# Delta attention on one core: the query sums move to TensorE, and the newest chunk's errors get a way of their own

## The chip, the cores and the metric

The program runs on one core of one Trainium2 chip, as one launch that computes eight sublayers in a row. The metric is the device time of the launch in microseconds (us). Engines are PE (TensorE), DVE (VectorE), ACT (ScalarE), POOL (GpSimd) and SP (SyncE, which issues the DMAs). All data of the stage in question is fp32.

## The reference, cut to what matters

The changed stage is the seventh sublayer, a gated delta rule. Per batch entry and head it carries a 128x128 state S through the sequence:

```
y   = S k_t                       # what the state answers to the key
err = y - v_t
S   = a_t * S - (b_t * err) k_t^T
o_t = S q_t                       # the output, read with the query
```

In this program the batch has 4 entries of 256 steps, and the width 256 is spread over 16 heads of 128, so there are 64 lanes (head x batch entry). k, q and v come from projections, a causal convolution of four taps and a SiLU; a and b are sigmoids. The outputs are normalized, gated and projected back.

## The kernel before, in words

`delta_attention` works in chunk form. The 256 steps are 4 blocks of 64 (`NBLK`); a block is two half-blocks of 32 steps (`NO`, index o), each of them four chunks of 8 steps (`NI`, index jj; `ci = o*NI + jj`). In a block come, in this order:

- heads: projections, convolution and SiLU for 16 heads, on PE, ACT, DVE and POOL, interleaved with the norm, gate and output projection of the block before (`heads_and_norm`);
- Gram matrices of keys with keys and queries (`gram`, L2046), scaled by -beta into GR (L2410), scattered to DRAM chunk by chunk and read back by SP in broadcast form into M, one of two rooms per chunk (L1853, L1863);
- for each half-block: transposing the state (`state_t`, L2058) and multiplying it with keys and queries (`columns`, L2068) into F (L2331), key rows (`key_rows`), then the four chunks, then the update of S (`update`, L2120, added by DVE in L2491).

For each chunk, POOL's `prepare` builds the decay products DD (L1976), DC, DF, scales F by them (L1999), subtracts V (L2000, semaphore `fp_d`) and multiplies the query half of M by DD (L2002, `mq_d`). Between two chunks it decays the errors W found so far (L2015, `wdec_d`). DVE's `chunk` multiplies the key half of M by DD (L2439), waits for `fp_d` and for `rest_mm`, forms the base in a PSUM bank (L2431, L2432; L2430 in the first chunk), and runs seven key steps of a product and an add (L2454, L2456), since each step's error depends on the earlier ones. It writes W (L2460, `w_d`), and then forms the outputs in bank 5: a base, and eight steps of a product (L2471) and an add (L2478). ACT copies bank 5 to V (L2379).

PE's part between two chunks is a turn (16 transposes of W, L2088, copied by ACT in L2351) and `rest` (L2101): 64 small matmuls, seen as 128 instructions, that carry all errors of the half-block so far to the next chunk's columns. `rest_mm` releases DVE's base of the next chunk.

Each engine runs its instructions in the order in which its function is written; engines meet only at the semaphores. Nothing is planned or scheduled by a table. In the second half-block of each block PE also computes four gate matrices per chunk (`gate`, L2131).

## Time and profile before

| | us |
|---|---|
| median of 3 runs | 2733.68 (2719.57 to 2734.51) |
| the profiled execution's own time | 2720.65 |
| its span, first to last instruction | 2718.9 |

The delta stage takes from about 986 to 2340 us of the span. The page's totals are over all eight sublayers. A row of a view names a source line, the engine, the operation, output and inputs with their shapes, how often it ran, its busy time and the mean of one, and what released the engine after its idle time. A matmul of fp32 shows as two instructions. The granted clock is a share of full speed: 1.00 is 2.4 GHz and 0.50 is 1.2 GHz.

### The profile page before, as it was taken

The numbers are of one execution on the slowest core, as the hardware profiler recorded it, in microseconds if no ns is written. First come the engines' busy times: TensorE is split into PE (matmuls) and PEld (weight loads), VectorE is DVE, ScalarE is ACT, GpSimd is POOL, SyncE is SP. The second block draws the span as 40 slices with busy tenths as digits, with TensorE's granted clock in tenths as the row PEclk, the third lists the DMA queues.
The fourth block names the chain that finished last, engine by engine and source line by source line (L and its number), as shares of the span: only waits on it lengthen the run. The fifth ranks groups of instructions, "written<-read, shape, count | busy, mean of one in ns | idle before, by whom it ended". The sixth has DMA issues, their size and how long they took to land. (4 is left out here: it accounts for less than half of the span.)

```text
span 2718.9 us, 42746 instructions
## 1 busy us (share of the span) xinstructions
PE 2081.5 (77%) x15844; PEld 1636.3 (60%) x15856; DVE 1592.5 (59%) x3191; ACT 1141.1 (42%) x2723; POOL 1175.9 (43%) x996
## 2 busy tenths in 40 slices
PE   7597449978988968657896578955689656768798
PEld 5364126656566857646776567755568655546586
DVE  2223732246664339668776787766778677546533
ACT  3112311136464428434464344743446434325433
POOL 0222022210004535968339683386733877300254
PEclk9698769979998979767797677976779757789899
DMA  8422022210007023422223222232222332020340
GB/s 282 125 24 53 0 69 43 24 38 2 22 2 231 0 34 109 126 95 94 86 74 125 96 94 86 74 119 101 94 77 80 111 114 93 32 56 2 93 138 15
DMA packets 137426, 212.96 MB, mean 78 GB/s; under 512 B 61184, under 2 KB 113680, under 8 KB 132112
## 3 DMA queue, kind: packets, MB, share of 16 engines
q1 hardware_dynamic: 129072, 200.11, 23.1%
q0 software_dynamic: 8160, 10.26, 2.4%
q8 instruction: 122, 2.00, 0.3%
q14 instruction: 72, 0.59, 0.1%
HBM read 187.97 MB, written 22.37 MB: 77 GB/s over the span
## 5 line engine op out<-in xcount | busy, mean ns | idle before, releaser
L2088 PE MATMUL PS<-ident,XT 128*128 128x128 f32 x512 | 112.8, 402 | 258.2 <-DVE XT L2460 245.5
L2402 DVE SCALAR_TENSOR_TENSOR XT<-M_delta,CW_delta,XT 128x256 f32<-128x256 f32 x576 | 249.9, 495 | 70.2 <-ACT M_delta L2271 40.6
L2088 PEld LDWEIGHTS PS<-ident,XT 128*128 128x128 f32 x512 | 90.4, 208 | 277.6 <-DVE XT L2460 132.7
L2037 PE MATMUL PS<-XP_delta,X 128*128 128x268 f32 (+1 forms) x1024 | 241.6, 388 | 5.5 <-DMA X<-in_L_attn_b_heads 5.5
L2037 PEld LDWEIGHTS PS<-XP_delta,X 128*128 128x128 f32 x1024 | 192.7, 189 | 55.7 <-issue 11.4
L1541 PE MATMUL PS<-XP_rffn,UW_rffn 128*128 128x512 f32 x816 | 194.6, 395 | 5.5 <-POOL UW_rffn L1495 4.6
L1976 POOL TENSOR_TENSOR DD_delta<-DD_delta,A_delta 128x64 f32<-128x64 f32 (+6 forms) x224 | 169.9, 759 | 39.2 <-ACT A_delta L2359 19.5
L1541 PEld LDWEIGHTS PS<-XP_rffn,UW_rffn 128*128 128x128 f32 x816 | 155.5, 191 | 39.5 <-issue 6.8
L1273 ACT ACTIVATE PR_attn<-PS,NM_attn 128x256 f32<-128x256 f32 (+1 forms) x384 | 130.7, 448 | 103.6 <-DVE NM_attn L1343 103.6
L1495 POOL TENSOR_TENSOR UW_rffn<-W_rffn,UW_rffn 128x512 fp32r<-128x512 f32 x34 | 44.1, 1298 | 296.0 <-ACT UW_rffn L1602 296.0
L561 POOL DMA_INDIRECT sums<-XS_moe,token_moe x46 | 71.7, 1559 | 221.0 <-ACT XS_moe L661 205.8
L2002 POOL TENSOR_TENSOR M_delta<-M_delta,DD_delta 128x2304 f32<-128x2304 f32 x32 | 164.9, 5154 | 0.0
L1663 DVE TENSOR_TENSOR SU_rffn<-PS,CB_rffn 128x512 f32<-128x512 f32 x68 | 47.0, 691 | 179.8 <-PE PS L1541 158.4
L2373 ACT ACTIVATE S_delta<-S_delta,AO_delta 128x128 f32<-128x128 f32 x512 | 152.0, 389 | 0.0
L2351 ACT COPY KQ_delta<-PS 128x512 f32<-128x512 f32 x128 | 73.3, 585 | 183.5 <-PE PS L2088 183.5
L2068 PE MATMUL PS<-KQ_delta,TR_delta 128*128 128x64 f32 x1024 | 137.7, 282 | 13.3 <-DVE TR_delta L2419 13.1
L2101 PEld LDWEIGHTS PS<-XN,KQ_delta 16*128 16x128 f32 (+2 forms) x3072 | 142.3, 284 | 7.1 <-issue 7.1
L2101 PE MATMUL PS<-XN,KQ_delta 16*128 16x16 f32 (+2 forms) x3072 | 144.9, 336 | 0.0
L2068 PEld LDWEIGHTS PS<-KQ_delta,TR_delta 128*128 128x128 f32 x1024 | 132.9, 203 | 17.6 <-DVE TR_delta L2419 17.6
L1504 POOL TENSOR_TENSOR HP_rffn<-HF_rffn,HP_rffn 128x512 fp32r<-128x512 f32 x68 | 92.7, 1381 | 115.9 <-ACT HP_rffn L1625 115.9
L1918 POOL TENSOR_SCALAR XT<-M_delta,CW_delta,CB_delta 128x256 f32<-128x256 f32 x64 | 51.7, 808 | 164.4 <-ACT M_delta L2271 164.4
L1343 DVE TENSOR_REDUCE NM_attn<-PS 128x4 f32<-128x512 f32 (+1 forms) x144 | 95.0, 684 | 47.3 <-PE PS L1155 47.3
(414 smaller groups left out, 5068.6 us busy)
## 6 DMA issues: line engine op xcount, KB each, us to landing
M_delta<-gram_delta SPq DMA_DIRECT2D x32, 2304.0 KB, 8.7
X<-in_L_attn_b_heads SPq DMA_DIRECT2D x64, 512.0 KB, 3.4
EW<-in_L_ffn_w SPq DMA_DIRECT2D x24, 512.0 KB, 10.0
CB_rffn<-routes_rffn SPq DMA_DIRECT2D x20, 512.0 KB, 22.4
XN<-in_L_attn_b_outs SPq DMA_DIRECT2D x16, 512.0 KB, 3.6
F_delta<-in_L_attn_b_outs SPq DMA_DIRECT2D x4, 2048.0 KB, 8.5
W_rffn<-in_L_ffn_tiles SPq DMA_DIRECT2D x4, 1536.0 KB, 11.6
slots<-pad SPq DMA_DIRECT2D x2, 2967.0 KB, 14.7
```

What stands on the lines that cost most here:

```text
L1273: last = nc.scalar.activation(PR[:, u % (2 * ROWS), j * w:(j + 1) * w], PS[:, r, j * w:(j + 1) * w], ACT.Exp, bias=NM[:, u % (2 * ROWS), j ...
L1343: nc.vector.tensor_reduce(NM[:, u % (2 * ROWS), 0:per], PS[:, r, :].rearrange("p (h j) -> p h j", h=per), AX.X, ALU.max, negate=True).then ...
L1504: nc.gpsimd.tensor_tensor(HP[1][:, r, x], HF[:, n, :], HP[0][:, r, x], ALU.subtract).then_inc(hl_d, 1)
L1541: last = nc.tensor.matmul(PS[:, 4 + 2 * n + q, :], UW[qw][:, r, (q * KD + k) * P:(q * KD + k + 1) * P], XP[qx][:, k, n * NB:(n + 1) * NB], ...
L1976: last = nc.gpsimd.tensor_tensor(DD[:, :, tri(t - 1) + 1:tri(t)], DD[:, :, tri(t):tri(t + 1)], step(t).broadcast_to([P, BH, C - t]), ALU.mult)
L2002: nc.gpsimd.tensor_tensor(q, q, by_h(DD[:]), ALU.mult).then_inc(mq_d, 1)
L2037: last = nc.tensor.matmul(PS[:, 1 + i, 0:B * (WIN - halo)], WH[:, r, i, k, :], XP[:, k, :, n * BT + halo:n * BT + WIN], start=(k == 0), st ...
L2068: last = nc.tensor.matmul(PS[:, 5 * (g % 2), i * 2 * OC:(i + 1) * 2 * OC].rearrange("p (q t) -> p q t", q=2), TR[:, g % 3, i * P:(i + 1) * ...
L2088: last = nc.tensor.transpose(PS[:, 6 + r % 2, i * P:(i + 1) * P], W[:, B * h:B * (h + 1), :], core.ident[:])
L2101: last = nc.tensor.matmul(PS[:, 1 + b, h * 2 * C:(h + 1) * 2 * C].rearrange("p (q t) -> p q t", q=2), WT(o)[rows, h, :], GR[rows, o, h].re ...
L2373: last = nc.scalar.activation(S[:, lane, :], S[:, lane, :], ACT.Copy, scale=AO[:, lane:lane + 1])
L2402: nc.vector.scalar_tensor_tensor(TMP[:, r, i], RAW[:, r, i, :, tau:tau + BT], CW[:, i, h, tau:tau + 1], TMP[:, r, i], ALU.mult, ALU.add).t ...
```

## The change

- DVE no longer adds up the outputs. Its eight products with the query half of M are written back into M, and PE sums them in bank 5 with identity matmuls (`add_steps`), behind two more that bring in F and the query term TQ (`add_first`). ACT copies the bank one chunk later (`answer`).
- The base of the queries (TQ) is formed by DVE ahead of the key steps.
- The errors of the newest chunk go to the next chunk by `newest`: DVE writes them to WN, PE turns them with four transposes, ACT copies them to NEW, and 16 matmuls multiply them with GN, a Gram matrix of one chunk's keys with the next chunk's keys and queries. GN is made once per half-block by `cross_gram` (48 matmuls on PE, three copies and twelve scalings on ACT), and POOL clears what belongs to other batch entries (`same_lanes`) before each use, so that it is block-diagonal.
- The turn and `rest` now handle only older chunks, for chunks 2 and 3, in banks that four matmuls first set to zero. `rest` runs in four tiers with a wait between them. There are three turns per half-block instead of four. ACT copies WN to W (`wc_d`).
- POOL still multiplies the query half of M by DD.
- beta is computed a second time in another layout at the start of the stage, stored to DRAM and read back. The scratch tiles of the norms become one tile.

```diff
+            def same_lanes(n, o, jj):
+
+                pool.wait_ge(cg_d, base_of(n)["cg_d"] + rests(o, jj) + 1)
+                g = GN[:, jj].rearrange("p (i b w) -> p i b w", i=4, b=B)
+                nc.gpsimd.tensor_tensor(g, g, SAME[:].unsqueeze(1).unsqueeze(3).broadcast_to([P, 4, B, 2 * C]),
+                                        ALU.mult).then_inc(gn_d, 1)
...
                     if jj:
-                        pool.wait_ge(wt_mm, z["wt_mm"] + NR * ci)
+                        pool.wait_ge(wc_d, z["wc_d"] + rests(o, jj))
                         r = W[:, :, 0:jj * C]
                         nc.gpsimd.tensor_tensor(r, r, AJ[:, :, jj:jj + 1].broadcast_to([P, BH, jj * C]),
                                                 ALU.mult).then_inc(wdec_d, 1)
                         pool.wait_ge(wdec_d, z["wdec_d"] + rests(o, jj))
+                    if jj + 1 < NI:
+                        same_lanes(n, o, jj)
...
             def rest(n, o, jj):
...
-                for h in range(H):
...
+                for k in range(4):
+                    nc.tensor.matmul(PS[:, 1 + k, 0:2 * C * H], XP[:, 0, 0, 0:1].broadcast_to([P, P]), XP[:, 0, 0, 0:2 * C * H],
+                                     start=True, stop=False)
+                pe.wait_ge(wt_d, z["wt_d"] + NR * (TURNS * o + jj - 1))
+                for y in range(4):
+                    if y:
+                        pe.wait_ge(tier, z["tier"] + 4 * (2 * o + jj - 2) + y)
...
+            def newest(n, o, jj):
+
+                z = base_of(n)
+                x = rests(o, jj - 1)
+                for i in range(4):
+                    last = nc.tensor.transpose(PS[:, 6, i * P:(i + 1) * P], WN[:, i * P:(i + 1) * P], core.ident[:])
+                last.then_inc(nw_mm, 1)
...
+                for i in range(4):
+                    for k in range(4):
+                        rows, at = slice(OC * k, OC * (k + 1)), slice(i * 2 * B * C, (i + 1) * 2 * B * C)
+                        last = nc.tensor.matmul(PS[:, 1 + k, at], NEW[rows, i], GN[rows, jj - 1, at], start=jj == 1,
+                                                stop=jj == 1 or i == 3)
                 last.then_inc(rest_mm, 1)
...
+            def add_steps(n, ci):
+
+                z = base_of(n)
+                for t in range(C):
+                    pe.wait_ge(qm_d, z["qm_d"] + C * ci + t + 1)
+                    last = nc.tensor.matmul(FQ[:, :, :, t:], core.ident[:], M[:, ci % 2, :, 1, :, tri(t):tri(t + 1)],
+                                            start=False, stop=t == C - 1)
+                last.then_inc(q_d, 1)
...
+                        if jj:
+                            add_steps(n, ci - 1)
+                        if 1 <= jj < NI - 1:
+                            pe.wait_ge(wdec_d, z["wdec_d"] + rests(o, jj))
+                            for r in range(NR):
+                                turn(n, TURNS * o + jj - 1, r)
+                            rest(n, o, jj + 1)
+                        add_first(n, ci)
                         pe.wait_ge(w_d, z["w_d"] + ci + 1)
...
-            cuts = [0, 0, 21, 42, BH]
+            cuts = [0, 20, 32, 44, BH]
...
                 dve.wait_ge(mq_d, z["mq_d"] + ci + 1)
...
+                for t in range(C):
+                    x = q[:, :, :, tri(t):tri(t + 1)]
+                    nc.vector.tensor_tensor(x, x, by_h(FK[:, :, t:t + 1].broadcast_to([P, BH, C - t])), ALU.mult).then_inc(qm_d, 1)
```

How the instructions stand on PE's queue between two chunks, before (L2088 is the turn, L2101 `rest`):

```order
L2078 MATMUL PS<-ident,KQ_delta 128x128 x16
L2088 MATMUL PS<-ident,XT 128x128 x16
L2101 MATMUL PS<-XN,KQ_delta 128x16 x64
L2088 MATMUL PS<-ident,XT 128x128 x16
L2101 MATMUL PS<-XN,KQ_delta 128x16 x64
```

And in the changed kernel, from the end of chunk 0's sums to the errors of chunk 1 (L2134 is the turn, L2163 the zeroing, L2174 `rest`, L2206 and L2209 `add_first`, L2185 and L2195 `newest`, L2216 `add_steps`):

```order
L2134 MATMUL PS<-ident,XT 128x128 x16
L2163 MATMUL PS<-XP_delta 128x256 x4
L2174 MATMUL PS<-XN,KQ_delta 128x16 x64
L2206 MATMUL PS<-F_delta,ident 128x512
L2209 MATMUL PS<-TR_delta,ident 128x512
L2185 MATMUL PS<-ident,TR_delta 128x128 x4
L2195 MATMUL PS<-GN_delta,TR_delta 128x64 x16
L2216 MATMUL PS<-M_delta,ident 128x512
L2216 MATMUL PS<-M_delta,ident 128x64x7
```

The matmuls that release the next chunk (L2195) come last, behind the turn, `rest` and the sums of F and TQ. On POOL's queue of the changed kernel, between the q product of chunk 1 and the decays of chunk 2, the masking of GN (L2007) is new, and nothing has gone:

```order
L2046 TENSOR_TENSOR M_delta<-M_delta,DD_delta 128x16x144
L2059 TENSOR_TENSOR XT<-XT,AJ_delta 128x64x8
L2007 TENSOR_TENSOR GN_delta<-GN_delta,SAME_delta 128x256
L2019 TENSOR_TENSOR DD_delta<-DD_delta,A_delta 128x64
L2019 TENSOR_TENSOR DD_delta<-DD_delta,A_delta 128x64x2
```

L2046 is the old L2002, L2059 the old L2015 and L2019 the old L1976.

## Rows read from the trace of the kernel before

**Rows 1.** The page: engine totals, and two of its groups (busy us, mean ns).

```profile
PE 2081.5 (77%) x15844; PEld 1636.3 (60%) x15856; DVE 1592.5 (59%) x3191; ACT 1141.1 (42%) x2723; POOL 1175.9 (43%) x996
...
L2351 ACT COPY KQ_delta<-PS 128x512 f32<-128x512 f32 x128 | 73.3, 585 | 183.5 <-PE PS L2088 183.5
...
L2101 PE MATMUL PS<-XN,KQ_delta 16*128 16x16 f32 (+2 forms) x3072 | 144.9, 336 | 0.0
```

**Rows 2.** Busy times in stretches: us, then busy us by engine, clock, DMA.

```profile
core 0: us, PE busy (x) PEld busy (x) DVE busy (x) ACT busy (x) POOL busy (x), PEclk, DMA share, GB/s
1110.00:1195.00 85.00, 36.34 (x521) 32.47 (x509) 76.16 (x145) 34.55 (x100) 80.78 (x59) 0.58 0.33 109
```

**Rows 3.** Groups of POOL in one period, 1130.90 to 1151.95 us (busy, mean; idle).

```profile
L1976 POOL TENSOR_TENSOR DD_delta<-DD_delta,A_delta 128x64 f32<-128x64 f32 (+6 forms) x7 | 5.3, 757 | 0.6
L2002 POOL TENSOR_TENSOR M_delta<-M_delta,DD_delta 128x2304 f32<-128x2304 f32 x1 | 5.1, 5074 | 0.0
L2000 POOL TENSOR_TENSOR F_delta<-F_delta,V_delta 128x512 f32<-128x512 f32 x1 | 3.5, 3454 | 0.1
L1999 POOL TENSOR_TENSOR F_delta<-F_delta,DF_delta 128x512 f32<-128x512 f32 x2 | 2.4, 1196 | 0.2
L1992 POOL TENSOR_TENSOR DF_delta<-DC_delta,PJ_delta 128x576 f32<-128x576 f32 x1 | 1.2, 1182 | 0.1
L1985 POOL TENSOR_TENSOR DC_delta<-DD_delta,A_delta 128x512 f32<-128x512 f32 x1 | 1.2, 1156 | 0.1
L2015 POOL TENSOR_TENSOR XT<-XT,AJ_delta 128x512 f32<-128x512 f32 x1 | 1.1, 1149 | 0.1
L1990 POOL TENSOR_TENSOR PJ_delta<-AJ_delta 128x64 f32<-128x64 f32 x1 | 0.3, 301 | 0.1
```

**Rows 4.** Groups of DVE in the same period.

```profile
L2478 DVE TENSOR_TENSOR PS<-PS,TR_delta 128x512 f32<-128x512 f32 (+7 forms) x8 | 3.7, 458 | 0.0
L2471 DVE TENSOR_TENSOR TR_delta<-M_delta,PS 128x512 f32<-128x512 f32 (+7 forms) x8 | 3.6, 462 | 0.0
...
L2431 DVE TENSOR_TENSOR PS<-PS,DC_delta 128x512 f32<-128x512 f32 x2 | 1.4, 695 | 1.2 <-POOL F_delta L2000 1.2
```

**Rows 5.** PE in order of time (start, length), then clock in two stretches.

```profile
1143.26 3.76 PE L2088 MATMUL PS<-ident,XT 128*128 128x128 f32 x16 [9.37 <-DVE XT L2460]
...
1234.79 3.72 PE L2131 MATMUL PS<-XP_delta,XN 128*128 128x256 f32 x16 [1.40 <-ACT KQ_delta L2345]
...
1288.63 7.03 PE L2101 MATMUL PS<-XN,KQ_delta 24*128 24x16 f32 x128
1295.59 6.74 PE L2131 MATMUL PS<-XP_delta,XN 128*128 128x256 f32 x16
...
1311.59 2.09 PE L2120 MATMUL PS<-KQ_delta 32*128 32x128 f32 x32
...
1316.28 1.17 PE L2120 MATMUL PS<-KQ_delta 32*128 32x128 f32 x32 [0.68 <-DVE S_delta L2491]
...
2270.26 3.76 PE L2101 MATMUL PS<-XN,KQ_delta 8*128 8x16 f32 x128
...
1246.00:1250.00 4.00, 4.00 (x80) 0.50 0.27 74
2270.00:2274.00 4.00, 4.00 (x133) 1.00 0.01 4
```

**Rows 6.** DVE in order of time at the ends of both half-blocks.

```profile
1185.51 0.69 DVE L2460 TENSOR_TENSOR XT<-PS,X 128x512 f32<-128x512 f32 x1
...
1198.31 2.29 DVE L2491 TENSOR_TENSOR S_delta<-S_delta,PS 128x2048 f32<-128x2048 f32 x1 [2.29 <-PE PS L2120]
...
1304.39 0.69 DVE L2460 TENSOR_TENSOR XT<-PS,X 128x512 f32<-128x512 f32 x1
...
1317.51 2.29 DVE L2491 TENSOR_TENSOR S_delta<-S_delta,PS 128x2048 f32<-128x2048 f32 x1 [1.38 <-PE PS L2120]
```

**Rows 7.** One line's instructions over the span: ns min/median/max.

```profile
L2000 POOL TENSOR_TENSOR F_delta<-F_delta,V_delta x32: 1250/1284/3474, 1111.5 to 2320.9; 128x512 f32<-128x512 f32 x32
L1958 POOL TENSOR_TENSOR X<-X,A_delta x56: 1101/1127/1162, 1095.5 to 2227.0; 128x256 f32<-128x256 f32 x56
```

More of the change, by code:

```diff
@@ L1694, in delta_attention @@
     NR = 4
+    TURNS = NI - 1
     PAIRS = C * (C + 1) // 2
@@ L1784, in _ @@
             last.then_inc(z_mm, 1)
+            for n in range(NH):
+                for k in range(KD):
+                    last = nc.tensor.matmul(PS[0:H, 1 + n, :], WB[:, k, :], XT[:, k, n * NB:(n + 1) * NB],
+                                            start=(k == 0), stop=(k == KD - 1))
+            last.then_inc(row_mm, 1)
         @block.scalar
@@ L1790, in _ @@
             nc.scalar.activation(NBETA[:], NBETA[:], ACT.Sigmoid).then_inc(beta_d, 1)
+            act.wait_ge(row_mm, 1)
+            for n in range(NH):
+                last = nc.scalar.activation(ZT[:, n * NB:(n + 1) * NB], PS[0:H, 1 + n, :], ACT.Sigmoid, bias=RT[0:H, 0:1])
+            last.then_inc(row_d, 1)
         @block.vector
@@ L2106, in rest @@
-                last.then_inc(rest_mm, 1)
+                for k in range(4):
[5 more added lines that the diff above has]
+                        pe.wait_ge(tier, z["tier"] + 4 * (2 * o + jj - 2) + y)
+                    for i in range(4):
+                        for k in range(4):
+                            h, b = 4 * k + i, (k + y) % 4
+                            rows = slice(OC * b, OC * b + (jj - 1) * C)
+                            at = (i * B + b) * 2 * C
+                            last = nc.tensor.matmul(PS[:, 1 + k, at:at + 2 * C].rearrange("p (q t) -> p q t", q=2),
+                                             WT(o)[rows, h, :],
+                                             GR[rows, o, h].rearrange("p (q t) -> p q t", q=2)[:, :, jj * C:(jj + 1) * C],
+                                             start=False, stop=False)
+                    last.then_inc(tier, 1)
@@ L2304, in heads_and_norm @@
                 if n:
+                    answer(n - 1, NC - 1)
                     square(n - 1, 0)
@@ L2371, in _ @@
                                                      ACT.Sigmoid).then_inc(gate_d, 1)
+                        if jj:
+                            answer(n, ci - 1)
+                        if 1 <= jj < NI - 1:
+                            for r in range(NR):
+                                turn(n, TURNS * o + jj - 1, r)
                         for lane in range(cuts[jj], cuts[jj + 1]):
```

246 lines of the change are left out of this document (158 added, 88 removed).

## The prediction, made before the changed kernel ran

> **What bounds the kernel now.** I read the page's engine totals first: over the span PE is the busiest engine, then DVE, POOL and ACT [rows 1]. Such totals mix eight sublayers, and the change lies in one of them, the delta attention. So I then read the busy times of a stretch of that stage, the four chunks of one half-block [rows 2]: there POOL works 80.8 of 85 us, DVE 76.2, PE 36.3, ACT 34.6. POOL and DVE run neck and neck, and the question is which of them sets the pace. The groups of one chunk answer it. The stretch of [rows 3] is one period of 21.05 us (from one subtraction L2000 to the next), and in it POOL's eight kinds of work fill 20.1 us, with some 0.1 us before each instruction and no releaser behind any of it: POOL waits for nobody. DVE waits 1.2 us in the same stretch, for POOL's L2000 [rows 4]. So POOL sets the period, with DVE 1.2 us behind. The wait for `fp_d` (F less V, from POOL) is the one that ends last at the start of each chunk.
>
> A second thing to see there is L2000 itself: 3454 ns in the chunk, 1250 at its shortest, for one shape [rows 3, 7]. The long ones lie beside DVE's L2439 (M times DD, both in SBUF). That is 2.2 us of POOL time per chunk, and the change keeps L2439.
>
> **The change, part by part.** There are 4 blocks of 2 half-blocks of 4 chunks, so 8 half-blocks and 24 intervals between chunks of one half-block.
>
> *DVE loses work.* Per chunk the eight adds of L2478 go (3.7 us) and one base add; the eight products of L2471 stay (3.6 us) [rows 4]; the query term is now one product (0.7 us, L2431's duration) that stands ahead of the key steps. DVE's chunk shrinks by some 4.4 us. Inside a half-block I cost this gain at nothing: it only lengthens the 1.2 us that DVE waits for POOL. What stays is that the errors of a half-block's last chunk come 0.7 us later after `fp_d`: 8 x 0.7 = **+5.6 us**.
>
> *POOL gains work.* After the q product it now masks GN (128x256, in place, one operand broadcast) in three of four chunks. No row has this operation. Half of L2015's 128x512, also in place with a broadcast, is 0.58 us [rows 3]; L1958, 256 elements with a stride, takes 1.13 [rows 7]. GN is contiguous, so I take 0.75. A new wait for `fp_d` ahead of the q product adds about 0.1, the idle time shown between other dependent POOL instructions [rows 3]. Since POOL sets the period, all of it is on the path: 24 x 0.85 = **+20.4 us**, ends +14 and +30. Nothing of POOL's old work is removed: L2002's 5.1 us stay.
>
> *PE gains work and a longer way.* The eight matmuls of gates (L2131, 2048 fp32 columns) give the price of a column: 3.72 us at the full clock, 6.74 at half of it [rows 5], so 1.8 or 3.3 ns. By it the identity sums of M (2304 columns) take 4.2 or 7.6 us, F and the query term (1024 columns) 1.9 or 3.4, and the four matmuls that zero the banks (1024) 1.9 or 3.4. What matters is the wait they end. The old way was W, 16 transposes, 128 instructions of `rest`, then the next chunk. Now the fresh errors take a short way (`newest`), but on PE's queue it stands behind the turn of the older ones, and this turn waits for POOL's `wdec_d` of the same chunk. From `wdec_d` to `rest_mm`: turn 3.8, zeros 1.9, `rest` 3.8, its three tier waits 1.0 (an estimate: each is the end of one matmul, near the 336 ns that one matmul of L2101 lasts on average [rows 1]), F and query term 1.9, four transposes 0.5, ACT's copy with hand-overs 0.9 [rows 1], 16 matmuls 1.2: 15.0 us at the full clock. At half it is 3.8 + 3.4 + 7.0 + 1.0 + 3.4 + 1.0 + 0.9 + 2.1 = 22.6 [rows 5]. POOL needs from the end of L2015 to the next `fp_d` 5.9 + 1.3 + 0.4 + 1.3 + 2.6 + 3.5 = 15.0 [rows 3], and 0.85 more now: 15.8. So at the full clock `rest_mm` is 0.8 us early, at half it is 6.8 late. In the second half-blocks gates (3.7 or 6.7) and the M sums (4.2 or 7.6) come between `newest` and the next turn, 7.9 or 14.3 us where POOL takes 7.2 (L2002 and L2015 of two chunks, 2.0): another 0.7 or 7.1. POOL itself does not wait for DVE's delay, so lateness does not add up from chunk to chunk; only that of the last chunk ends up in the time. The granted clock stood at 0.50 in one such stretch and at 1.00 in another with the same instructions [rows 5]; the 24 `rest` runs took 144.9 us [rows 1], 6.0 each, so most ran at half. The denser PE should hold the full clock longer. I take 2 us late per half-block: **+16 us**, ends 0 and 8 x 6.8 + 4 x 7.1 = +83.
>
> *Ends of half-blocks.* Before, the second state update on DVE (L2491) starts 12.8 us after the last L2460 in a first half-block, 13.1 in a second [rows 6]. Now DVE is free 3.6 us sooner, but ACT may turn W only after the answer of the chunk before and after 20 state lanes, and PE puts the 4.2 us of M sums between the first update and the second. In first half-blocks the turn is copied 5.5 us after the last error product, the sums end at 10.0, the second update's matmuls at 11.2, so 4 x -1.6 = **-6.4**. For second ones the last block's output also waits for the sums and ACT's copy before the norm can start: +2.1 for three, +4 for the last, **+10**. A PE that comes warm into the updates does one in 1.17 instead of 2.09 us [rows 5], and the transposes behind it too: **-8**, ends 0 and -24.
>
> *Once, at the start.* A second product for beta, 4 matmuls of 512 columns (3.7 to 6.7 us, the price of L2131's 2048 [rows 5]), two sigmoids, a reordering multiply and a store that the stage waits for: about **+9**, ends 8 and 12. The Gram matrices of neighbouring chunks (48 small matmuls, 12 ACT scalings, three copies per half-block, 7 us on ACT) stand ahead of ACT's key rows. What hides them is POOL's product of F and q for chunk 0 and DVE's key steps; if this cover were gone they would cost up to 7 us x 8. I take 0. A copy of W by ACT (`wc_d`) ends with `rest_mm` and POOL asks for it 5 us after `fp_d`: 0.
>
> Sum: 5.6 + 20.4 + 16 - 6.4 + 10 - 8 + 9 = **+47 us** on the profiled execution's 2720.65, so 2768. The three runs shown have a median of 2733.68, 13 us above that execution; on it the same sum gives 2781. Between these I forecast **2770 us**.
>
> Here a rule speaks otherwise. The Trainium skill (Perfetto Trace Analysis, Identifying the Most-Contended Engine) says to relieve the engine with the highest occupancy first. Over the span that is DVE before POOL, and the change would be right; for the stretch itself the rule picks POOL, which gains work. The measured idle times decide for the second reading.
>
> **The rivals.**
> A, faster: DVE's chain is the pace, and POOL's records only look closed because spans on POOL are rough. Then the period falls by 4.4 us in 24 intervals: 2720.65 - 106 + 9 = 2624 us. For it: DVE works 76.2 of 85 us [rows 2]. Against: 1.2 us of DVE idle, always released by L2000. It decides if POOL can deliver `fp_d` in under 20 us. 5%.
> B, PE at half clock: `rest_mm` late by the 6.8 to 14 us above. With half of the bound +83, no gain in the updates and a slower start: 5.6 + 20.4 + 42 - 6.4 + 10 + 0 + 12 = +84, so 2805, up to 2850 with all of it. For it: the low clock in most `rest` runs. Against: the PE now idles far less. 22%. The Trainium skill (TensorE: Matmul & The Clock Gate, Part 4: PE-mode transpose) says that transposes do not count as activity that raises the clock; by it the turn would start each `rest` at the low clock, which is this rival. No row before shows the new mix.
> C, nearly nothing: the full clock everywhere, masking at its low end: 5.6 + 14 + 0 - 6.4 + 10 - 16 + 8 = +15, so 2736 to 2749. 25%.
> D, the shortcut does not shorten: `newest` waits behind `rest` on PE's queue. This is in my sum already.
>
> **Numbers.** My forecast has 48%, with a range of its own of 2750 to 2800. The range that holds 8 in 10 takes in C and most of B: 2732 to 2825. About 1% (27 us) is what a measurement of this kernel tells from no change. Above 2761 lie two thirds of the forecast and B: 0.56. C, the rest of the forecast and a little of A's neighbourhood are within 1%: 0.37. Faster: 0.07.
>
> **What would show it.** POOL closed from chunk to chunk, the `fp_d` period about 0.85 us longer (21.9 and 22.8 us), DVE's wait at the chunk's start grown from 1.2 to 4 or 5 us, the first base product released by POOL in chunk 1 and in part by PE (newest matmuls) in chunks 2 and 3, and a granted clock above 0.58 in the first halves. I am wrong if POOL shows gaps, if its masking takes over 1.2 us, or if ACT's Gram work delays the key rows into the first chunk.

## The result, and the profile of the changed kernel

The changed kernel takes 2811.77 us (median of 4 runs, 2809.05 to 2814.28); the kernel before took 2729.41 beside it. The ratio is 1.031 (95% interval 1.027 to 1.034): slower by some 82 us, where I had forecast 2770, from a sum of 47 us on the profiled execution. The profiled execution took 2814.28 us with a span of 2812.4, 93.5 more than that of before.

To see where they lie I divided the stage at the starts of DVE's error products, the last instruction of each chunk's recursion (L2460 before; L2624, and L2628 in a half-block's last chunk, after). An error product here is the instruction that writes W or WN; a time written W + x is x us after the start of the last one of a half-block. The stage runs from SP's store of `spill` to its reload.

| us, sums over the stage | before | after | difference | forecast |
|---|---|---|---|---|
| start to the first error product | 135.8 | 148.9 | +13.1 | +9 |
| chunks 0 to 3 in 4 first half-blocks | 251.4 | 275.5 | +24.1 | +21 |
| from there to chunk 0 of the second | 224.1 | 221.6 | -2.5 | -11 |
| chunks 0 to 3 in 4 second half-blocks | 253.5 | 289.5 | +36.0 | +21 |
| 3 block ends | 479.1 | 490.3 | +11.1 | +3 |
| the last one | 62.6 | 70.3 | +7.7 | +4 |
| stage | 1406.5 | 1496.0 | +89.5 | +47 |

The forecast column deals my terms out: 24 x 0.85 + 8 x 0.7 + 8 x 2 = 42 for the chunks in two equal halves, and the -8 for the clock evenly over the seven ends before the last. The last block's end is the stretch from its last error product to the reload. The other 4 us of the span lie outside the stage, 2 on each side.

Busy times in the first half-block, which answer to [rows 2]. The stretch starts 4.9 us before the end of chunk 0's subtraction on POOL, as that one does:

```profile
1125.00:1210.00 85.00, 62.16 (x627) 43.87 (x616) 59.17 (x109) 37.22 (x121) 80.68 (x59) 0.79 0.30 98
```

PE has gone from 36 to 62 us of 85, DVE from 76 to 59, and POOL is where it was (80.8, now 80.7). So far this is the picture I expected. What released DVE at the start of a chunk shows the difference: this is the wait in front of the first base product. In the kernel before, over all chunks (engine, output, line, releaser: us in all, times, longest):

```profile
DVE PS L2431 <- POOL F_delta L2000: 39.5, 22, 2.4
```

And after, the same product, now L2606, and the product of M ahead of it (L2592):

```profile
DVE PS L2606 <- PE PS L2195: 116.0, 20, 9.0
DVE M_delta L2592 <- DMA M_delta<-gram_delta: 56.2, 12, 8.3
DVE PS L2606 <- POOL F_delta L2042: 25.0, 4, 6.3
```

POOL's subtraction came last in 22 chunks; now it does in 4, and in 20 it is PE's `newest` (L2195). I had expected DVE to be released "by POOL in chunk 1 and in part by PE (newest matmuls) in chunks 2 and 3". Most of those 116 us DVE would have waited for POOL in any case. What PE costs is how far the base product starts behind the end of POOL's subtraction. In the kernel before, this is 0.03 to 0.11 us in chunks 1 to 3 (2.3 in one). Now, in us over the four blocks:

| base behind POOL's subtraction | chunk 1 | chunk 2 | chunk 3 |
|---|---|---|---|
| after, first half-blocks | 0.1 | 0.2 to 0.8 | 2.5 to 2.6 |
| after, second half-blocks | 0.7 to 1.6 | 6.0 to 8.2 | 6.3 to 7.9 |
| e1, second half-blocks | 0.1 | 0.9 to 1.1 | 1.9 to 2.5 |
| e3, second half-blocks | 0.1 | 0.1 to 1.1 | 1.2 to 3.7 |

(e1 and e3 are runs below: without the gates, and with ACT's work moved.) One of them, chunk 2 of the first block's second half-block:

```profile
1291.05 1.25 POOL L2042 TENSOR_TENSOR F_delta<-F_delta,V_delta 128x512 f32<-128x512 f32 x1
1299.95 0.70 DVE L2606 TENSOR_TENSOR PS<-PS,DC_delta 128x512 f32<-128x512 f32 x1 [3.24 <-PE PS L2195]
```

In first half-blocks the intervals are 21.7, 22.1 to 22.6 and 24.5 to 25.1 us, where before they were 20.2, 21.0 and 22.0. POOL is closed there, as forecast, its subtractions 21.8 to 22.0 and 22.7 to 22.9 us apart, and its new masking is as small as assumed:

```profile
L2007 POOL TENSOR_TENSOR GN_delta<-GN_delta,SAME_delta 128x256 f32<-128x256 f32 x24 | 14.7, 613 | 1.9
```

The second half-blocks have 22.3, 26.5 and 23.4 us (or 23.0, 24.3, 24.9). POOL's subtractions of chunks 0 and 3 lie 63.7 to 64.7 us apart there, no more than the 64.8 to 65.3 of first half-blocks: POOL does not slow down with the others. Here is ACT in chunk 0 of such a half-block, whose error product starts at 1259.81, in order of time:

```profile
1264.44 0.38 ACT L2519 ACTIVATE KQ_delta<-PS 128x256 f32<-128x256 f32 x1 [0.48 <-PE PS L2243]
1264.72 5.93 ACT L2527 ACTIVATE S_delta<-S_delta,AO_delta 128x128 f32<-128x128 f32 x20
1270.56 0.56 ACT L2534 COPY TR_delta<-PS 128x512 f32<-128x512 f32 x1
```

And PE, from the transposes of the newest errors on (L2243 gates, L2216 sums, L2134 turn, L2163 zeroing, L2174 `rest`, L2206 and L2209 `add_first`):

```profile
1265.84 0.60 PE L2185 MATMUL PS<-ident,TR_delta 128*128 128x128 f32 x4
1271.27 1.99 PE L2195 MATMUL PS<-GN_delta,TR_delta 32*128 32x64 f32 x32 [4.83 <-ACT TR_delta L2534]
...
1273.19 5.28 PE L2243 MATMUL PS<-XP_delta,XN 128*128 128x256 f32 x16
1278.94 4.72 PE L2216 MATMUL PS<-M_delta,ident 128*128 128x512 f32 x16 [0.47 <-ACT KQ_delta L2519]
1283.48 1.06 PE L2134 MATMUL PS<-ident,XT 128*128 128x128 f32 x8
1284.83 1.15 PE L2134 MATMUL PS<-ident,XT 128*128 128x128 f32 x8 [0.29 <-ACT KQ_delta L2475]
1285.81 1.89 PE L2163 MATMUL PS<-XP_delta 128*128 128x256 f32 x8
1287.63 6.21 PE L2174 MATMUL PS<-XN,KQ_delta 8*128 8x16 f32 x128
1293.78 2.08 PE L2206 MATMUL PS<-F_delta,ident 128*128 128x512 f32 x2
1295.64 1.63 PE L2209 MATMUL PS<-TR_delta,ident 128*128 128x512 f32 x2
1297.11 0.60 PE L2185 MATMUL PS<-ident,TR_delta 128*128 128x128 f32 x4
1298.68 1.12 PE L2195 MATMUL PS<-GN_delta,TR_delta 32*128 32x64 f32 x32 [0.97 <-ACT TR_delta L2534]
```

ACT scales the state S of 20 lanes (L2527, "state lanes" below) before it copies the turned errors, so PE stands for 4.8 us. From then on PE's queue has hardly a gap: gates, sums, turn, zeroing, `rest`, `add_first` and the next `newest` take 27 us, and 23.4 in the chunk behind it. The errors of chunk 1 are ready at 1282.8, but their transposes start at 1297.1. The same lanes stand ahead of the last turn at a block's end, whose error product is at 1332.10:

```profile
1332.61 5.96 ACT L2527 ACTIVATE S_delta<-S_delta,AO_delta 128x128 f32<-128x128 f32 x20
1338.46 1.05 ACT L2475 COPY KQ_delta<-PS 128x512 f32<-128x512 f32 x2
```

### The profile page after: what moved, and what is told of

The parts are those of the page before. It is cut to its first block and busy times, and to the rows that moved or that the text cites. A ratio compares the mean times of both kernels' runs of the same rounds, so it can differ in the third digit from the quotient of the medians.

```text
span 2812.4 us, 45244 instructions
## 1 busy us (share of the span) xinstructions
PE 2301.0 (82%) x17096; PEld 1727.1 (61%) x17096; DVE 1460.2 (52%) x2913; ACT 1186.3 (42%) x2933; POOL 1195.3 (43%) x1020
## 3 DMA queue, kind: packets, MB, share of 16 engines
q1 hardware_dynamic: 129664, 200.24, 22.6%
## 5 line engine op out<-in xcount | busy, mean ns | idle before, releaser
L2046 POOL TENSOR_TENSOR M_delta<-M_delta,DD_delta 128x2304 f32<-128x2304 f32 x32 | 181.9, 5685 | 11.7 <-DMA M_delta<-gram_delta 9.8
L2019 POOL TENSOR_TENSOR DD_delta<-DD_delta,A_delta 128x64 f32<-128x64 f32 (+6 forms) x224 | 170.1, 759 | 34.9 <-ACT A_delta L2507 19.5
L2216 PE MATMUL PS<-M_delta,ident 128*128 128x256 f32 (+7 forms) x512 | 166.3, 482 | 5.7 <-ACT KQ_delta L2519 5.7
L2527 ACT ACTIVATE S_delta<-S_delta,AO_delta 128x128 f32<-128x128 f32 x512 | 153.0, 392 | 0.0
L2216 PEld LDWEIGHTS PS<-M_delta,ident 128*128 128x128 f32 x512 | 97.0, 204 | 75.8 <-issue 53.9
L2640 DVE TENSOR_TENSOR S_delta<-S_delta,PS 128x2048 f32<-128x2048 f32 x28 | 64.0, 2287 | 102.5 <-PE PS L2232 102.5
L2592 DVE TENSOR_TENSOR M_delta<-M_delta,DD_delta 128x2288 f32<-128x2288 f32 x32 | 84.5, 2640 | 61.6 <-DMA M_delta<-gram_delta 56.2
L2134 PE MATMUL PS<-ident,XT 128*128 128x128 f32 x384 | 67.4, 334 | 56.4 <-POOL XT L2059 26.3
## 6 DMA issues: line engine op xcount, KB each, us to landing
CB_rffn<-routes_rffn SPq DMA_DIRECT2D x20, 512.0 KB, 22.7
```

Source lines behind the costliest of these rows:

```text
L2019: last = nc.gpsimd.tensor_tensor(DD[:, :, tri(t - 1) + 1:tri(t)], DD[:, :, tri(t):tri(t + 1)], step(t).broadcast_to([P, BH, C - t]), ALU.mult)
L2046: nc.gpsimd.tensor_tensor(q, q, by_h(DD[:]), ALU.mult).then_inc(mq_d, 1)
L2216: last = nc.tensor.matmul(FQ[:, :, :, t:], core.ident[:], M[:, ci % 2, :, 1, :, tri(t):tri(t + 1)], start=False, stop=t == C - 1)
L2527: last = nc.scalar.activation(S[:, lane, :], S[:, lane, :], ACT.Copy, scale=AO[:, lane:lane + 1])
L2592: nc.vector.tensor_tensor(k[:, :, 1:], k[:, :, 1:], DD[:].rearrange("p (h b) w -> p h (b w)", b=B)[:, :, 0:B * PAIRS - 1], ALU.mult).then_ ...
```

## The experiments

**Theory after the result.** (1) In second half-blocks PE is late: the state lanes on ACT delay it in chunk 0, and its queue, with the gates in it, is too long to catch up. (2) The block ends wait for the same lanes. (3) In first half-blocks POOL sets the pace, and PE comes a little behind. (4) The start is the second computation of beta. **Rival:** POOL, with its masking and the new wait, sets the pace everywhere, or the sums on PE are the cost by themselves. The same sections of the stage, for every kernel (us; one profiled execution each). Ratios below are to the kernel before, run beside each kernel. The profiled executions of e1, e3, e5, e6 and e7 are the shortest of their runs and that of after the longest of its four, so the columns of these five lie some us lower against after than their ratios do:

| | start | first | between | second | 3 ends | last | stage |
|---|---|---|---|---|---|---|---|
| before | 135.8 | 251.4 | 224.1 | 253.5 | 479.1 | 62.6 | 1406.5 |
| after | 148.9 | 275.5 | 221.6 | 289.5 | 490.3 | 70.3 | 1496.0 |
| e1 no gates | 144.9 | 272.8 | 220.7 | 273.1 | 489.2 | 69.6 | 1470.2 |
| e2 mask on DVE | 154.6 | 255.2 | 239.7 | 268.9 | 500.7 | 70.3 | 1489.3 |
| e3 lanes moved | 146.7 | 274.0 | 223.2 | 270.5 | 477.4 | 62.5 | 1454.2 |
| e4 sums only | 137.1 | 256.5 | 221.0 | 256.4 | 473.6 | 61.5 | 1406.1 |
| e5 no beta row | 134.8 | 266.2 | 217.0 | 294.1 | 497.8 | 67.2 | 1477.1 |
| e6 sums late | 146.4 | 274.5 | 229.4 | 288.7 | 500.3 | 70.4 | 1509.7 |
| e7 q on DVE | 138.1 | 245.8 | 225.6 | 238.5 | 479.6 | 61.7 | 1389.3 |
| e8 before, more POOL | 134.6 | 257.3 | 234.3 | 260.2 | 479.0 | 66.4 | 1431.8 |
| e9 lanes, no row | 135.3 | 268.0 | 223.9 | 272.6 | 484.6 | 65.7 | 1450.1 |
| e10 cheap zero | 147.9 | 274.0 | 218.9 | 273.7 | 479.1 | 65.7 | 1459.2 |
| e11 zero, mask 1, 2 | 147.6 | 265.3 | 217.8 | 275.2 | 487.5 | 65.8 | 1459.3 |
| e12 products early | 137.9 | 245.5 | 249.6 | 253.1 | 479.5 | 61.3 | 1426.9 |

**e1: the gates left out.**

```diff
-                for k in range(KD):
-                    last = nc.tensor.matmul(PS[:, 6 + h % 2, 0:B * BT], WG[:, h % 4, k * P:(k + 1) * P], ...
+                last = nc.tensor.matmul(PS[:, 6 + h % 2, 0:B], WG[:, h % 4, 0:P], XP[:, 0, :, n * BT + TAPS - 1],
+                                        start=True, stop=True)
...
-                                nc.scalar.activation(GATES[:, h // 2, h % 2], PS[:, 6 + h % 2, 0:B * BT],
+                                nc.scalar.activation(GATES[:, h // 2, h % 2, 0:B], PS[:, 6 + h % 2, 0:B],
```

> The changed kernel with its gates reduced to one matmul of 4 columns per head (16 per block; the gate values are wrong, so the output is too). Theory (in second half-blocks PE's own queue is the loop that sets the pace, gates 3.7 to 5.3 us of it): the three chunk intervals of a second half-block fall from 72.3 us to about POOL's 68.8, 4 x -3.5, and at the block ends the sums, the answer and the 20 state lanes come 4 us sooner, 4 x -4: about 2782 us, 30 less than 2812. Rival (POOL's masking and its wait set the pace in both kinds of half-block): the second half-blocks stay at 72 us and the time within 8 us of 2812.

Measured: ratio 1.028 (1.025 to 1.031), 2795.3 us. The second half-blocks fall by 16.4 us in all, 4.1 each, and the base of their chunk 3 comes 1.9 to 2.5 us behind POOL's subtraction instead of 6.3 to 7.9, with POOL's masking still in place: PE's queue was their bound, and POOL was not. The block ends give nothing back, against my number: with the gates gone the lanes start 7 us earlier (at 1325.2), but the error product does nearly so too (1325.7), and the distance between them hardly changes. The ratio shows less (0.3% or 7 us, intervals overlap) than the 26 us of the stage in the profiled executions. By its time alone this run would fit the rival, which allowed 8 us; what decides against it is the second half-blocks, which did not stay at 72 us.

**e3: the lanes moved.**

```diff
-            cuts = [0, 20, 32, 44, BH]
+            cuts = [0, 8, 36, BH]
...
-                        for lane in range(cuts[jj], cuts[jj + 1]):
+                        for lane in range(cuts[jj], cuts[jj + 1]) if jj < NI - 1 else ():
...
+                        if jj == NI - 2:
+                            last.then_inc(sdec_d, 1)
                         if jj == NI - 1:
-                            last.then_inc(sdec_d, 1)
                             for r in range(NR):
```

> The changed kernel with ACT's 64 state lanes cut 8, 28, 28, 0 over the four chunks instead of 20, 12, 12, 20. Theory: ACT's copy of the turned errors no longer waits for lanes in chunk 0 of the second half-blocks (PE stood 4.8 us there; its queue starts 3 to 4 us sooner and so does all that follows), nor do the copies of the last turn at the block ends (3.3 us) and half-block ends (0.9 us): 4 x 3.5 + 4 x 3.3 + 4 x 0.9 = 31 us back, 2781. Rival (ACT is off the path, PE or POOL takes over at once): within 8 us of 2812.

Measured: 1.019 (1.017 to 1.022), 2773.9 us: 0.0112 less than after, 30 us, the 31 of the theory. The profiled stage gives back 41.8 us: 19.0 in the second half-blocks, 12.9 in the block ends, 7.8 in the last one; the ends of first half-blocks show nothing. In second half-blocks the base of chunk 3 is now 1.2 to 3.7 us behind POOL's subtraction. DVE's waits at L2607 (the same product) now stand thus:

```profile
DVE PS L2607 <- PE PS L2195: 74.2, 13, 9.7
DVE PS L2607 <- POOL F_delta L2042: 60.3, 11, 6.3
```

The clock has a part in it, and this run does not separate it from the pause. In after, the stretches of PE's queue behind the 4.8 us pause ran at 0.68 and 0.70 (gates, `rest`), and in e3 the same ones at 1.00, with 3.72 us for the gates instead of 5.28 and 4.58 for `rest` instead of 6.21, together 3.2 of the 7.65 us by which that chunk's base was late. After, then e3:

```profile
1271.70:1278.90 7.20, 6.77 (x48) 5.40 (x44) 5.24 (x9) 1.75 (x6) 7.04 (x3) 0.68 0.01 2
1287.60:1293.80 6.20, 5.95 (x130) 5.58 (x129) 0.00 (x0) 2.50 (x9) 4.47 (x4) 0.70 0.83 297
```

```profile
1263.90:1269.10 5.20, 4.75 (x48) 3.86 (x48) 1.39 (x2) 2.17 (x8) 4.96 (x4) 1.00 0.01 3
1278.20:1282.70 4.50, 4.24 (x130) 3.92 (x129) 1.95 (x7) 4.50 (x17) 4.13 (x5) 1.00 0.89 333
```

**e2: the masking done by DVE**, in `chunk` ahead of its wait for `fp_d`; the call of `same_lanes` on POOL goes.

```diff
-                    if jj + 1 < NI:
-                        same_lanes(n, o, jj)
...
+                if jj + 1 < NI:
+                    dve.wait_ge(cg_d, z["cg_d"] + rests(o, jj) + 1)
...
+                    nc.vector.tensor_tensor(g, g, SAME..., ALU.mult).then_inc(gn_d, 1)
                 dve.wait_ge(fp_d, z["fp_d"] + ci + 1)
```

> The changed kernel with the masking of GN (0.61 us on POOL, three chunks in four) done by DVE while it waits for fp_d. Theory: in first half-blocks POOL's loop gets 0.7 us shorter per chunk, but PE's newest matmuls are already 0.8 and 2.6 us behind fp_d there and take over, so less than 12 x 0.7 = 8 us comes back; in second half-blocks nothing: 2804 to 2812. Rival (POOL sets the pace everywhere): 24 x 0.7 = 17 us back, 2795.

Measured: 1.029 (1.027 to 1.031), which on the 2729 of after's measurement is 2808, in the theory's range by its sum and not by its parts. The chunks give back 41 us, and 34 are lost between half-blocks, at the ends and at the start. In chunk 0 DVE now waits for ACT's Gram matrix, and then runs the masking beside POOL's product of M (L2046, 1127.98 to 1133.06), ahead of the key steps:

```profile
1130.77 2.57 DVE L2604 TENSOR_TENSOR GN_delta<-GN_delta,SAME_delta 128x256 f32<-128x256 f32 x1 [3.97 <-ACT GN_delta L2491]
```

So the cover that my prediction named for the Gram work was real: without it, the Gram work and the masking behind it cost 3.5 to 6 us per half-block (5.7 at the start, 4.5 in each gap, 3.5 at each block end), and the base of chunk 0 starts 5.4 us behind POOL's subtraction in seven of eight half-blocks. What it shows of POOL's masking alone is blurred, since a later chunk 0 also shortens the first interval (18.2 us).

**e4: the sums alone.** The kernel before with `add_first`, `add_steps` and `answer`, the in-place products on DVE and TQ ahead of the key steps; turn and `rest` as before.

> The kernel before with one part of the change alone: PE adds the query sums, DVE forms TQ ahead of the key steps. Turn and rest as before, four per half-block; no Gram matrix of neighbouring chunks, no masking, no second beta; the state lanes stand ahead of the gates and the answer on ACT. Theory: POOL's loop is unchanged (21.05 us), so chunk intervals stay at 63.3 us per half-block and DVE only waits longer; the ends of blocks give some us back or take some: 2720 to 2745. Rival (the sums on PE are the cost by themselves, 4.7 us per chunk): second half-blocks grow by 5 to 9 us each and the time is 2755 to 2780.

Measured: 1.002 (1.0005 to 1.004), 2726.1 us; the rival falls. The chunk intervals are 20.9, 21.1 and 22.2 us, and POOL comes last in all 24 of them, with DVE waiting up to 6.7 us:

```profile
DVE PS L2479 <- POOL F_delta L2003: 99.7, 24, 6.7
```

Thus half of the change is free and worth nothing: it takes 4.4 us per chunk from an engine that then waits. Nearly all of the 82 us comes with the rest of the change: the errors' new way and what it needs, the second beta included.

**e8: the kernel before with one product more on POOL**, 128x256 with a broadcast, in three of four chunks:

```diff
                         pool.wait_ge(wdec_d, z["wdec_d"] + rests(o, jj))
+                    if jj + 1 < NI:
+                        pool.wait_ge(chain_m, count)
+                        nc.gpsimd.tensor_tensor(more, more, MANY..., ALU.mult).then_inc(chain_m, 1)
```

> The kernel before with one product more on POOL in three of four chunks, of the size and shape of the masking (128x256 in place, on tiles that nobody else uses). Theory (POOL sets the pace in every chunk before): 24 x 0.7 = 17 us more, ratio 1.006. Rival (DVE sets it or covers it): no more than 4 us, ratio below 1.002.

Measured: 1.008 (1.006 to 1.011). The product takes 0.61 us in the median, and nearly every interval grows by 0.5 to 0.6 us, 12.6 in all by the table; POOL did set the pace. Another 10 us stand between the half-blocks, in two of four gaps (58.5 and 63.4 us instead of about 55) with a clock of 0.69 in the longest; what lowered it there was not tried.

**e5: no second beta.** A constant is stored at the start of the stage.

```diff
-            sp.wait_ge(c_in, CIN)
             sp.wait_ge(turned_d, 1)
             sp.dma_start(bdram, ZP).then_inc(row_out, 16)
+            sp.wait_ge(c_in, CIN)
...
+            nc.gpsimd.memset(ZP, -0.5).then_inc(turned_d, 1)
```

The matmuls, the sigmoids and the multiply of the second beta go as well.

> The changed kernel without its second computation of beta: the 4 matmuls, the two sigmoids and the reordering multiply are left out, and a constant is stored at the very start of the stage and read back as before (the Gram matrices of neighbouring chunks are scaled wrongly). Theory: the store is off the path, so the chain of matmuls 6.2, sigmoids 1.3, multiply 1.1 and the store's wait, 10.4 us of later DMA of the heads in the profiles, comes back: about 10 us less than the changed kernel. The four small loads of 2.4 us stay. Rival (the 15 us come from elsewhere in the heads, such as the slower norm or the small loads on SP's queue): within 4 us of the changed kernel.

Measured: 1.030 (1.026 to 1.033). The first error product comes 134.8 us after the stage's start, as before the change, so all 13 to 14 us were this chain. In after it reads thus on PE, SP (where L1773 is the store) and PE again:

```profile
1011.62 6.24 PE L1799 MATMUL PS<-XT,WB_delta 128*16 128x512 f32 x8
```

```profile
1020.34 0.33 SPq L1773 DMA_DIRECT2D beta_delta<-A_delta  x1
1023.40 1.00 SPq L1877 DMA_DIRECT2D X<-in_L_attn_b_heads  x2
```

```profile
1028.47 2.15 PE L2083 MATMUL PS<-XP_delta,X 128*128 128x268 f32 x4 [10.61 <-DMA X<-in_L_attn_b_heads]
```

The ratio, though, hardly shows it (0.1% below after), and in the profiled execution two second half-blocks took 75 us instead of 72. Hence the same edit once more, where the second half-blocks have slack:

**e9: lanes moved and no second beta** (both edits).

> The two edits that answered best, together: state lanes cut 8, 28, 28, 0, and the second computation of beta left out (a constant is stored and read back instead, so GN is scaled wrongly). Theory: the start of the stage and its half-blocks have nothing to do with each other, so on top of the 1.019 with the lanes moved, 13 us (0.5%) go: ratio about 1.0145, and the first error product of the stage comes 135 us after the spill's store, as in the kernel before, instead of 147 to 149. Rival (what the start gives back is lost again behind it): ratio 1.019.

Measured: 1.0153 (1.0128 to 1.0178), 0.0041 below e3, 11 us, and again the first error product after 135.3. The two intervals still overlap a little; the stage's start itself leaves no doubt.

**e6: the sums behind the second update.**

```diff
-                            if r == 0:
+                            if r == 1:
                                 add_steps(n, NI * (o + 1) - 1)
```

At the block ends the same order is made: the second update's matmuls, then the sums.

> The changed kernel with the last chunk's sums behind the second state update's matmuls on PE instead of ahead of them. Theory (the 5.5 us of sums stand in the way of the second update, which starts at W3 + 13.6 instead of the 11.2 I forecast): the second update comes 4 to 5 us sooner, the sums then delay the transposes of the new state by some 2 us: 2 to 4 us back per first half-block, 4 x 3 = 12, and 0 to 4 us in three block ends: 12 to 24 us less. Rival (DVE's adds and the state copies set the pace there, the order on PE is indifferent): within 5 us of the changed kernel.

Measured: 1.043 (1.040 to 1.046), slower by 1.2% of after, and the theory is wrong. The second update does come 2.1 us sooner (11.5 us after the error product), but three of the four gaps between half-blocks grow by 3.6 us, and the block ends by 3.3. (The profiled execution is the shortest of its six; its stage is 13.7 us longer than that of after, the ratio says 33.) PE, in order:

```profile
1209.84 2.09 PE L2232 MATMUL PS<-KQ_delta 32*128 32x128 f32 x32 [2.57 <-DVE S_delta L2639]
1211.86 6.71 PE L2216 MATMUL PS<-M_delta,ident 128*128 128x512 f32 x16
1219.33 1.07 PE L2104 MATMUL PS<-ident,S_delta 128*128 128x128 f32 x8 [0.77 <-ACT V_delta L2499]
```

The gap ends with the transposes of the new state (L2104), which stand behind the sums on PE's queue and wait for ACT's copy of them (`answer`, V). They start 18.8 us after the error product, against 13.5 in after. Where the change has the sums, half of them lies in the time that PE waits for DVE's first add anyway.

**e10: cheaper zeroing**, on top of e3.

```diff
-                    nc.tensor.matmul(PS[:, 1 + k, 0:2 * C * H], XP[:, 0, 0, 0:1]..., XP[:, 0, 0, 0:2 * C * H], start=True, stop=False)
+                    nc.tensor.matmul(PS[:, 1 + k, 0:2 * C * H], NIL..., NIL..., start=True, stop=False)    # bf16
```

> The changed kernel with the lanes moved, and the four matmuls that zero the banks before rest done with bf16 zeros instead of fp32 ones (same result; a fp32 matmul runs in more passes, so I expect 0.5 us or so instead of 1.9). Theory: PE's newest matmuls are 0.7 us behind fp_d in chunk 2 and 1.5 in chunk 3 of every half-block (intervals 22.6 and 24.5 where POOL's loop and DVE's extra 0.7 make 21.9 and 23.0), and this edit takes 1.4 us off PE's queue in each: 8 x 2.2 = 17 us less than with the lanes moved alone, ratio 1.013. Rival (PE has room there and POOL alone sets 22.6 and 24.5): no change, ratio 1.019.

Measured: 1.020 (1.018 to 1.023), no gain; the chunks take what they took in e3, or 3 us more. This looks like the rival (PE has room there), but it does not show it. Zeroing and `rest` ahead of one chunk 3 in e3, then in e10:

```profile
1526.94 3.12 PE L2163 MATMUL PS<-XP_delta 128*128 128x256 f32 x8
1529.99 5.80 PE L2174 MATMUL PS<-XN,KQ_delta 16*128 16x16 f32 x128
```

```profile
1531.62 1.06 PE L2167 MATMUL PS<-NIL_delta 128*128 128x256 bf16 x4
1532.61 7.89 PE L2178 MATMUL PS<-XN,KQ_delta 16*128 16x16 f32 x128
```

Zeroing falls from 3.1 to 1.1 us and `rest` rises from 5.8 to 7.9. The granted clock of the stretch behind the zeroing was 0.74 in e3 and 0.50 in e10:

```profile
1530.00:1536.00 6.00, 5.76 (x130) 5.42 (x130) 3.58 (x2) 5.96 (x21) 5.69 (x5) 0.74 0.11 6
```

```profile
1532.60:1538.00 5.40, 5.22 (x93) 5.01 (x92) 4.60 (x9) 5.40 (x20) 5.09 (x5) 0.50 0.52 167
```

With fewer long matmuls in front the clock rose later, and the small matmuls paid what the large ones had saved. It is so in three of the four first half-blocks ahead of chunk 3 (8.8 to 8.9 us from the zeroing's start to the end of `rest` in e3, 8.9 in e10), and there the base stayed 2.7 us behind POOL's subtraction. Over all 16 places it is milder: zeroing falls from 2.19 to 0.77 us in the mean, `rest` rises from 5.34 to 5.91, and both together fall from 7.47 to 6.80. So where chunk 3 waited for PE, PE's way was not shortened, and why the rest of the gain is not seen in the time stays open.

**e11: e10, and the masking for chunks 2 and 3 on DVE.**

> As the run with cheap zeroing, and the masking of GN for chunks 2 and 3 done by DVE in its wait at the start of chunks 1 and 2; that for chunk 1 stays on POOL. Theory: with PE in time, POOL's loop is what is left, and it loses 0.7 us in two of three intervals: 16 x 0.7 = 11 us less than with cheap zeroing, ratio 1.009, intervals 21.7, 21.2, 22.3. Rival (PE is still last): no change from the run with cheap zeroing.

Measured: 1.019 (1.017 to 1.022). The first half-blocks give back 8.7 us, 1.1 for each of the 8 intervals that lost a masking: there POOL's loop counts. The second ones give nothing, and one block end took 168 us. The forecast of 11 us over e10 failed: by the ratio 3 us came back, which is what the rival said, and PE came last in 14 chunks, as in e10.

**e7: towards a better kernel.** e4 with DVE multiplying the query half of M by DD, and the gates behind the sums.

```diff
+                q = M[:, ci % 2, :, 1]
+                nc.vector.tensor_tensor(q, q, by_h(DD[:]), ALU.mult).then_inc(mq_d, 1)
```

> Sums alone (as in the run before with PE's sums) and two moves more: DVE multiplies the query half of M by DD right behind the key half (some 2.5 us), POOL no longer does (5.1 us), and PE's gates stand behind the sums. Theory: POOL's loop falls from 21 to 16 us and no longer sets the pace; DVE's chunk (base 2.1, key steps 7.3, W 0.7, query products 3.1, two products of 2.5 each, waits) takes 19 to 20 us, and the turn and rest run beside the last of it: intervals of about 20 us, 24 x -1.2 = 29 us less than with the sums alone, about 2695. Rival 1: the next M arrives late, since its load waits for the sums (W + 14 us, plus 10.4 of DMA): 21 us intervals, no gain. Rival 2: as PE's turn and rest after W set the pace with 10 us: 20.5 us intervals, 2710.

Measured: 0.998 (0.996 to 1.000), 2715.7 us, against 1.002 for e4: 0.4% or 11 us better, where I expected 29. Most intervals did fall, to 20.4 in first half-blocks (21.8 in one) and between 18.3 and 22.2 in second ones, 29 us over the stage; 12 of them were lost at its ends. Two rows tell why no more came:

```profile
L2470 DVE TENSOR_TENSOR M_delta<-M_delta,DD_delta 128x2304 f32<-128x2304 f32 x32 | 119.7, 3741 | 0.0
```

```profile
L2004 POOL TENSOR_TENSOR F_delta<-F_delta,V_delta x32: 1252/3431/6062, 1110.7 to 2298.9; 128x512 f32<-128x512 f32 x32
```

DVE's product takes 2.55 us where POOL rests and 3.7 in the mean, and POOL's subtraction 3.4 in the median instead of 1.3. Here are the two side by side:

```profile
1130.70 3.55 DVE L2470 TENSOR_TENSOR M_delta<-M_delta,DD_delta 128x2304 f32<-128x2304 f32 x1
1131.91 3.46 POOL L2004 TENSOR_TENSOR F_delta<-F_delta,V_delta 128x512 f32<-128x512 f32 x1
```

The Trainium skill (SBUF — State Buffer, SBUF: two separate sides) says that a DVE operation with two inputs in SBUF and a GpSimd operation that reads SBUF lock each other out of a shared port, the later one for the whole instruction of the earlier. The rows agree: the subtraction, which takes 1.25 us alone, ends at 1135.37, 1.1 us after DVE's product. My second rival, PE's turn and `rest` behind the errors, is not excluded: in this chunk `rest` ended at 1135.30, 0.1 us ahead of the subtraction, and the rival's 20.5 us intervals and 2710 us are nearer to what was measured than the theory's 2695. It is the best of the kernels here, but by too little to tell it from the kernel before.

**e12: its products for a second half-block's chunk 0 between the state updates.**

> The sums alone with the query product on DVE and the gates behind the sums (0.998 of before), and DVE's two products of M with DD for the second half-block's first chunk done between the state updates, where DVE waits for PE, instead of behind them. Theory: in that run POOL's two products of F took 4.4 us beside them instead of 2.5, and now they stand alone: 4 x 2 = 8 us less, ratio 0.995. Rival (the gap between half-blocks is set by PE's updates and transposes, which the products now delay by up to 5 us): ratio 1.000 to 1.005.

Measured: 1.004 (1.002 to 1.006), the rival. The gaps between half-blocks grew by 6 us each, and the second half-blocks by 3.6.

## Why the prediction was right in sign and wrong in size

**The bound of the kernel before: right.** POOL's loop set it. Lengthening it lengthens the intervals (e8), relieving DVE alone gives nothing (e4). What I wrote of the rule of highest occupancy was incomplete: over the span PE (77%, its weight loads 60%) stood ahead of both DVE (59%) and POOL (43%), so the totals did not pick DVE either.

**POOL's 20.4 us: about right, somewhat too large.** 0.61 us for the masking, against 0.75 assumed; about 1 us per interval came back when it went (e11, first half-blocks). POOL's subtractions of chunks 0 and 3 moved apart by some 2.5 us in first half-blocks and 1.5 in second ones, where I had 2.55 in both: about 16 us in all.

**Query term, 8 x 0.7: right.** From the base's start to the error product it is 8.7 us instead of 8.1 in chunks 1 to 3, in after as in e4, which has no masking.

**PE's lateness, +16: the step that failed.** By the table above the bases of the eight last chunks start 38.5 us in all behind POOL's subtraction, 10.2 in first half-blocks and 28.3 in second ones. I wrote: "POOL itself does not wait for DVE's delay, so lateness does not add up from chunk to chunk; only that of the last chunk ends up in the time." The first half is true (POOL's subtractions lie no further apart in second half-blocks than in first ones), but `rest_mm` comes from PE's queue, and PE does not forget. Its instructions between one `newest` and the next form a loop of their own. In second half-blocks I had put it at 15.0 from `wdec_d` plus 7.9, that is 22.9, against POOL's 23.0, and called it "another 0.7 or 7.1". At the full clock it measured 23.4 (from one `newest` to the next, 1298.68 to 1322.12), so the size was nearly right, and such a loop has no slack to make up a delay: it carries it on. The delay was there too: 20 state lanes ahead of ACT's copy in chunk 0, which I had counted at the half-block's end and not here. The pause was followed by a low clock (0.68 and 0.70), and chunks 2 and 3 had the base's start 7.6 and 6.3 us behind `fp_d` instead of 2. In first half-blocks, where PE has 3.7 us less to do, 2 us was nearly right: 2.5 to 2.6. There it is mostly the clock: zeroing and `rest` ahead of chunk 3 took 8.8 us in all four, against 6.4 where the clock stood at 1.00. Either way out works, no gates (e1, -16 us) or no lanes (e3, -19).

**Ends, +10 - 6.4 - 8: wrong by 20 us, the second step that failed.** The lanes again: I had them ahead of the turn at a half-block's end, but gave the block ends only 2.1 us each for the later output. Without them there, 20.7 us go from the block ends (e3). For half-block ends I had the sums at 4.2 us and they took 5.76, behind an update of 2.09; the second update's add came at W + 13.6 instead of 11.2. The gaps between half-blocks fell by 1.1 us (54.9 to 53.8) where neither kernel has an outlier, against 2.6 forecast; each has one long gap, of 59.2 and 60.3 us.

**The clock, -8: little of it, and none in first half-blocks.** The clock rose, from 0.58 to 0.79 in the first half-block and from 0.830 to 0.879 over the span, as forecast. Of the 28 updates 10 took 2.09 us where 15 did before. But the first update of a first half-block, 1.17 to 1.38 us before, now takes 2.09 in all four, since PE waits ahead of it, and so what the second gains there (1.17 instead of 2.09) is lost again.

**Start, +9: too small.** +13.1, all of it the second beta (e5, e9). The matmuls ran at 6.24 us, near the upper of my two values, and from the store to the first DMA of the heads it was 3.1 us more; my sum gave no piece its own number.

**Key rows and Gram, 0: right,** with the cover named; e2 took it away and paid 3.5 to 6 us per half-block.

**The rivals.** The time is in the range of B (2805 to 2850), and the low clock, B's mechanism, has a share: 2.4 us ahead of chunk 3 in first half-blocks, and the 3.2 us in the chunk above. It is not the main one. Gates and `rest` ahead of chunk 3's base ran at 1.00 in after, with the turn right ahead of `rest`, and the base still started 6.3 us late:

```profile
1299.70:1303.90 4.20, 3.75 (x20) 2.89 (x16) 3.80 (x6) 1.53 (x4) 4.04 (x3) 1.00 0.01 4
1312.60:1317.10 4.50, 4.24 (x129) 3.93 (x128) 0.00 (x0) 2.49 (x9) 4.24 (x4) 1.00 0.90 327
```

A and C did not come. That my wide range (2732 to 2825) holds the time is owed to B, whose mechanism gave only a part of it: that is luck. None of the three signs of error that I named came either: POOL's only gaps between chunks are waits of up to 2.0 us for M's DMA, the masking takes 0.61 us, and chunk 0's base starts 0.1 us behind POOL's subtraction, so the key rows are not late. The failure lay where I had named no sign.

**Left open:** how the 4.8 us of pause and the low clock behind it share the lateness of chunk 2; why e10's shorter zeroing brought no time; the longer second half-blocks of e5, where the base of chunk 2 is 10.5 us late in two of them; the low clock in some gaps between half-blocks.

## What to carry to other kernels

For each engine add up all that its queue does between one hand-over and the next, other stages' work included, and compare that loop with the pace: here it took 23.4 us, no less than the pace of 22.7 to 22.9 us that POOL keeps between chunks 2 and 3, and a late start in the first turn was carried to the last. When a result gets a short way of its own, follow it through every in-order queue it crosses; here it stood behind 20 instructions on ACT that nobody was in a hurry for, and moving them gave back 30 of 82 us. And taking work from an engine that waits is worth nothing (e4): look for the edit that shortens the one waited for.

## What the runs showed of the hardware

- Replacing four fp32 zeroing matmuls by bf16 ones (2.19 to 0.77 us in the mean of 16 places) made the 128 small matmuls behind them slower, 5.34 to 5.91 us, so about half of the gain was left. In three places nothing was left (8.8 to 8.9 us before and after); in the one looked at, the small matmuls ran at a granted clock of 0.50 instead of 0.74 (e3, e10).
- Moving a 5.1 us product from POOL to DVE, where it takes 2.55 alone, made it 3.7 us there in the mean and POOL's subtraction 3.4 in the median instead of 1.3 (e7).
- The masking product of 256 elements took 0.61 us on POOL (after); on DVE it took 0.52 us at its shortest, 1.4 in the median, and 2.57 beside POOL's product of M (e2).
